# DLRM tower: one one-hot pick of 256 columns for two tiles, and six tiles of single-row fetches on SyncE

## The chip, the cores and the metric

One core of one Trainium2 chip. The metric is the device time of one execution in microseconds; the runs of the kernel before have a median of 560.53 us. Below, PE is TensorE, DVE is VectorE, ACT is ScalarE, POOL is GpSimd and SP is SyncE.

## What is computed

A recommendation tower over a batch of 2048 samples. Each sample has 27 ids; each id takes one row of 128 floats from its own table. The 27 rows, all 351 dot products between two different rows, and 16 dense values go through three layers in float32.

```python
def reference(dense_ctx, ids, tbl_0, ..., tbl_26, W_top1, b_top1, W_top2, b_top2, W_top3):
    e = jnp.stack([tbl_0[ids[:, 0]], ..., tbl_26[ids[:, 26]]], axis=1)   # 2048 x 27 x 128
    inter = jnp.einsum('bfd,bgd->bfg', e, e)[:, _TRIU_I, _TRIU_J]        # 351 pairs
    h = jnp.concatenate([e.reshape(B, -1), inter, dense_ctx], axis=1)    # 3823 wide
    h = jnp.maximum(h @ W_top1 + b_top1, 0.0)                            # 512
    h = jnp.maximum(h @ W_top2 + b_top2, 0.0)                            # 256
    return h @ W_top3
```

## The kernel before

The batch is cut into 16 tiles (0 to 15) of 128 samples. A tile has 9 groups of 3 features (FEATS = 3, GROUPS = 9). For each group the work goes through four engines:

- **POOL** gathers the rows of one feature for 128 samples with one indirect DMA (L320). The result goes to a ring of 6 group slots (RING), so a group's gathers may start once the group six places earlier has been transposed (L317). POOL does nothing else.
- **PE** transposes the three 128x128 blocks into a PSUM bank (L638), two items ahead of the item whose layer 1 it computes. It adds the group's part of layer 1 in three passes (L668 to L670): each float32 operand is split in a high and a low part of type float32r, and high x high, high x low and low x high are summed. Layer 1 of an item waits for the split (`group_low_done`).
- **ACT** writes the high part (L344) and a whole copy for the pair products (L351).
- **DVE** subtracts to get the low part (L469).

The order of the items is written out by hand: SEQUENCE is groups 0 to 6, then "pairs" (the interactions of the tile before), then groups 7 and 8. So the transposes of group 8 stand on PE in front of the layer 1 of "pairs". The pair products (L735), layer 2 and the last layer of earlier tiles are spread between the items. The last tile has a sequence of its own. p_group has two banks of four 128-column places, of which a group uses three.

Not all rows come through POOL:

- Feature 26 (PICKED) has a table of 1000 rows, which lies split in SBUF. For tiles 2 to 14 DVE compares the tile's 128 ids with the row numbers (`make_pick`, L543, once a tile), which gives a one-hot matrix of 1000 x 128, and PE multiplies the table with it in 16 matmuls of 128 columns (L625, L626), in front of the transposes of group 8.
- Feature 25 (FETCHED) comes through SP in the tiles 5, 8, 11 and 14 (FETCH_TILES). SP loads 16 ids into registers (L272), then issues 16 DMAs of one row each (L276), and so on for 128 rows. A tile's rows are split into three parts of 48, 48 and 32 rows, issued in three successive tiles' time (FETCH_PARTS), into one of two buffers (`fetched`). PE transposes them last in group 8 (L642), behind the wait for `rows_fetched`.

SP's queue runs in its written order. It loads the weights in 34 pieces through STAGES = 4 staging buffers; piece n waits until n - 3 pieces have been split (`w_low_done`, L245). Then for each tile from 2 on, it issues the load of the dense values (`load_ctx`, L261, which waits for `ctx_used` of an earlier tile), the load of the tile's ids for the pick (`load_pick_ids`, L279), and one part of the row fetches:

```python
            for t in range(PICK_FROM, TILES):
                load_ctx(t)
                if t < LAST:
                    load_pick_ids(t)
                if (t - 2) // 3 < len(FETCH_TILES):
                    fetch_rows((t - 2) // 3, (t - 2) % 3)
```

"(t, g)" below means group g of tile t.

Of the kernel before, what the change touches and what calls it, by code (L numbers as in the profile page):

```python
# [30 lines left out]
def dlrm_tower(nc, ids, ids_rows, fetch_ids, table_row, tables, ctx_rows, w_dense, w_pairs, b1_t, w2, b2, w3, eye, out):  # L31
# [27 lines left out]
    WIDE = NF + WRAP  # L59
    STAGES = 4  # L60

# [9 lines left out]
    picked_t = ids_rows.rearrange("(t b) -> t b", b=P)  # L71

    FETCHED = NF - 2
    FETCH_TILES = [5, 8, 11, 14]
    FETCH_PARTS = [0, 48, 96, P]
    FETCH_ROWS = tables[FETCHED].shape[0]
    LOADED = 16

    def picked_in(t):
        return PICK_FROM <= t < LAST  # L80

    def gathers_in(t, g):
        return FEATS - (g == GROUPS - 1) * (picked_in(t) + (t in FETCH_TILES))

# [4 lines left out]
    with ExitStack() as ctx:  # L89
# [19 lines left out]
        with ExitStack() as late:  # L109
            def later(name, shape, dt):  # L110
                return late.enter_context(nc.sbuf_tensor(name, shape, dt))

            pick = later("pick", [PICK_ROWS, PICK_CHUNKS, P], F32R)
            pick_ids = [later(f"pick_ids_{k}", [PICK_ROWS, P], I32) for k in range(2)]
            hid2 = later("hid2", [P, HID2], F32)
        stage_room = sb("stage_room", [P, STAGES, HID1])
        table_high = sb("table_high", [PICK_ROWS, PICK_CHUNKS, D], F32R)
        table_low = sb("table_low", [PICK_ROWS, PICK_CHUNKS, D], F32R)
        fetched = sb("fetched", [P, 2, D])
        table_row_sb = sb("table_row_sb", [PICK_ROWS, PICK_CHUNKS], I32)  # L120

# [20 lines left out]
        y = sb("y", [P, P])  # L142
        y_rows = sb("y_rows", [TILES, P])

# [11 lines left out]
        ctx_loaded = [sem(f"ctx_loaded_{k}") for k in range(2)]  # L156
        pick_ids_loaded = [sem(f"pick_ids_loaded_{k}") for k in range(2)]
        y_stored = sem("y_stored")
# [52 lines left out]
        def bank_of(t, n):  # L211
            return p_group[ORDER.index((t, n)) % 2][:, 0:FEATS, :]

        def occupant_before(t, n):
            return ORDER[ORDER.index((t, n)) - 2]
# [26 lines left out]
        def _(sp):  # L242
# [17 lines left out]

            def load_ctx(t):  # L261
                wait(sp, ctx_used, t - 1)
                sp.dma_start(ctx_sb[:, t % 2, :], ctx_t[:, t, :]).then_inc(ctx_loaded[t % 2], 16)
# [15 lines left out]
            def load_pick_ids(t):  # L279
                wait(sp, pick_done, t - PICK_FROM - 1)  # L280
                sp.dma_start(pick_ids[t % 2][:], picked_t[t].partition_broadcast(PICK_ROWS)).then_inc(
                    pick_ids_loaded[t % 2], 16)

            sp.dma_start(idx[:, 0:1, :], ids_t[:, 0:1, :]).then_inc(ids_loaded[0], 16)
# [12 lines left out]

            sp.wait_ge(w_low_done, len(STAGED))
            for t in range(PICK_FROM, TILES):
                load_ctx(t)  # L300
# [9 lines left out]
        def _(pool):  # L310
            pool.wait_ge(ids_loaded[0], 16)
            for t in range(TILES):
                if t == 1:
                    pool.wait_ge(ids_loaded[1], 16)
                for g in range(GROUPS):
                    slot = ring_slot(t, g)
                    wait(pool, group_transposed, t * GROUPS + g - RING + 1)  # L317
                    for k in range(gathers_in(t, g)):
                        f = g * FEATS + k
                        pool.indirect_dma_start(  # L320
                            gathered[:, slot, k, :], None, tables[f],
                            bass.IndirectOffsetOnAxis(ap=idx[:, t, f:f + 1], axis=0),
                        ).then_inc(group_gathered[slot], 16)

        @block.scalar
        def _(act):
            def weight_high(n):
# [11 lines left out]
                nc.scalar.activation(dst, src, ACT.Copy).then_inc(w_high_done, 1)  # L339

            def copy_high(t, g):
                s = t * GROUPS + g
                wait(act, group_used, s - SPLIT + 1)
                nc.scalar.activation(emb_high[:, s % SPLIT, :, :], bank_of(t, g),  # L344
                                     ACT.Copy).then_inc(group_high_done, 1)

            def copy_whole(t, g):
                if g == 0:
                    wait(act, round_done, (t - 1) * ROUNDS)
                f0 = g * FEATS  # L350
                nc.scalar.activation(emb[t % 2][:, :, f0:f0 + FEATS].rearrange("p b f -> p f b"),  # L351
                                     bank_of(t, g), ACT.Copy).then_inc(group_copied, 1)

            def group_copies(t, g):
# [7 lines left out]
                else:  # L362
                    copy_high(t, g)
                    copy_whole(t, g)

            def copy_first(t, r):
# [48 lines left out]
            for k, (t, n) in enumerate(ORDER):  # L415
# [28 lines left out]
        def _(dve):  # L444
# [17 lines left out]
            def group_low(t, g):  # L462
                s = t * GROUPS + g
                if t == 0:
                    for n in range(FEATS * g, FEATS * (g + 1)):
                        weight_low(n)
                dve.wait_ge(group_high_done, s + 1)
                dve.wait_ge(group_copied, s + 1)
                nc.vector.tensor_tensor(emb_low[:, s % SPLIT, :, :], bank_of(t, g),  # L469
                                        emb_high_f32[:, s % SPLIT, :, :], ALU.subtract).then_inc(group_low_done, 1)  # L470

# [63 lines left out]

            def make_pick(t):

                dve.wait_ge(pick_ids_loaded[t % 2], ((t - PICK_FROM) // 2 + 1) * 16)
                dve.wait_ge(w_low_done, len(STAGED))
                wait(dve, pick_used, t - PICK_FROM)  # L540
                rows = table_row_sb[:].unsqueeze(2).broadcast_to([PICK_ROWS, PICK_CHUNKS, P])
                ids_b = pick_ids[t % 2][:].unsqueeze(1).broadcast_to([PICK_ROWS, PICK_CHUNKS, P])
                nc.vector.tensor_tensor(pick[:], ids_b, rows, ALU.is_equal).then_inc(pick_done, 1)  # L543

# [16 lines left out]
            for k, (t, n) in enumerate(ORDER):  # L561
# [43 lines left out]
        def _(pe):  # L605
# [10 lines left out]
            def landings(t, g):  # L616

                groups = range((t * GROUPS + g) % RING, t * GROUPS + g + 1, RING)
                return sum(gathers_in(n // GROUPS, n % GROUPS) for n in groups)

            def pick_rows(t, dst):

                pe.wait_ge(pick_done, t - PICK_FROM + 1)
                for c in range(PICK_CHUNKS):
# [5 lines left out]
            def transpose_group(t, g):  # L630

                slot = ring_slot(t, g)
                wait_for_bank(t, g)
                if g == GROUPS - 1 and picked_in(t):
                    pick_rows(t, bank_of(t, g)[:, FEATS - 1, :])
                pe.wait_ge(group_gathered[slot], landings(t, g) * 16)
                for k in range(gathers_in(t, g)):
                    last = nc.tensor.transpose(bank_of(t, g)[:, k, :], gathered[:, slot, k, :], identity[:])  # L638
# [33 lines left out]
            def layer1_group(t, g, feats=range(FEATS)):  # L672
                s = t * GROUPS + g
                if g == 0:
                    wait(pe, hid1_copied, t - 1)
                pe.wait_ge(group_low_done, s + 1)
                for k in feats:
# [3 lines left out]
                    last = three_passes(p_hid1[t % 2][:], emb_high[:, s % SPLIT, k, :], emb_low[:, s % SPLIT, k, :],  # L681
                                        w1_high[:, f, :], w1_low[:, f, :], f == 0, False)
                if feats[-1] == FEATS - 1:
# [167 lines left out]
```

## Time and profile before

| | |
|---|---|
| Median of 3 runs | 560.53 us (556.34 to 561.19) |
| The profiled execution | 559.26 us |
| Its span, first to last instruction | 557.5 us |
| PE busy | 522.9 us (94%) |
| POOL busy | 399.2 us (72%) |
| ACT busy, DVE busy | 255.6 us (46%), 243.9 us (44%) |
| Gathers on POOL, single-row fetches on SP | 415, 512 |

The profile is of one execution. Its span is shorter than its device time by 559.26 - 557.5 = 1.8 us, which lie around the first and the last instruction. Busy time of PE is time in which at least one matmul was in flight; since matmuls overlap, the distance between the starts of two of them says what one costs. A matmul that waits shows as idle time in front of it. SP shows only when it issues: its row in the timeline merges issues of one line and gives their count. The page writes the names of buffers without their numbers.

### The profile page before, as it was taken

What the parts mean: (1) busy time and instruction counts of PE and PEld (TensorE: products, weight loads), DVE (VectorE), ACT (ScalarE), POOL (GpSimd) and SP (SyncE); (2) the same over time, 40 slices, a digit from 0 to 9 for tenths busy, and PEclk for the clock granted to TensorE, in tenths of its full rate; (3) what the DMA queues carried; (4) which work ended last, traced back from release to release, by engine and by line L of the source; (5) the groups of instructions that cost most, each with busy time, mean ns of one, the idle gap of its engine ahead of it and who ended that gap; (6) DMA issues with size and microseconds to landing.
All of it is one profiled execution on the core that took longest, in us unless ns stands there. A gap on an engine that the chain in (4) does not pass through costs nothing.

```text
span 557.5 us, 12647 instructions
## 1 busy us (share of the span) xinstructions
PE 522.9 (94%) x4420; PEld 429.9 (77%) x4420; DVE 243.9 (44%) x491; ACT 255.6 (46%) x488; POOL 399.2 (72%) x419
## 2 busy tenths in 40 slices
PE   0769889999999999999999999999999999999996
PEld 0547668878788788888888888888888888888884
DVE  3563533436254352534435253443525344352544
ACT  3674545353353535435353543535354353533542
POOL 6777777777777777777777777777777777777600
PEclk9998999999999999999999999999999999999999
DMA  6784321212112112211212121221212122111100
GB/s 171 257 256 130 110 54 57 57 54 60 53 56 59 55 54 56 60 54 57 59 54 59 54 59 54 58 61 55 59 54 59 53 57 60 55 53 54 53 2 1
DMA packets 27041, 38.80 MB, mean 70 GB/s; under 512 B 12455, under 2 KB 16504, under 8 KB 26978
## 3 DMA queue, kind: packets, MB, share of 16 engines
q0 software_dynamic: 13280, 27.22, 17.6%
q1 hardware_dynamic: 13698, 10.77, 6.7%
q8 instruction: 35, 0.57, 0.4%
q14 instruction: 28, 0.23, 0.1%
HBM read 37.96 MB, written 0.01 MB: 68 GB/s over the span
## 4 chain that ended last, share of the span: by engine, by line
PE 72%; POOL 17%; issue 6%; DMA 3%; ACT 1%; DVE 0%; DVEq 0%; ACTq 0%; POOLq 0%
POOL gathered L320 17%; PE p_hid L668 17%; PE p_hid L670 16%; PE p_hid L669 16%; PE p_prod L735 10%; PE p_group L638 7%; DMA gathered<-tbl_dram,idx 3%; PE p_group L626 1%; PE p_group L625 1%; PE p_hid_t L700 1%; PE p_group L655 1%; DMA idx<-ids_dram 0%; ACT emb L351 0%; PE p_hid L735 0%; PE p_hid_t L735 0%
## 5 line engine op out<-in xcount | busy, mean ns | idle before, releaser
L320 POOL DMA_INDIRECT gathered<-tbl_dram,idx x415 | 399.0, 961 | 128.5 <-issue 118.9
L668 PE MATMUL p_hid<-w_high,emb_high 128*128 128x512 f32 x432 | 183.6, 425 | 0.0
L670 PE MATMUL p_hid<-w_high,emb_low 128*128 128x512 f32 x432 | 171.0, 396 | 0.0
L669 PE MATMUL p_hid<-w_low,emb_high 128*128 128x512 f32 x432 | 169.7, 393 | 0.0
L469 DVE TENSOR_TENSOR emb_low<-p_group,emb_high 128x384 fp32r<-128x384 f32 x144 | 80.3, 558 | 195.3 <-ACT emb L351 194.8
L344 ACT ACTIVATE emb_high<-p_group 128x384 fp32r<-128x384 f32 x144 | 70.7, 491 | 161.3 <-PE p_group L638 145.3
L351 ACT ACTIVATE emb<-p_group 128x384 f32<-128x384 f32 x144 | 125.4, 871 | 0.0
L638 PE MATMUL p_group<-identity,gathered 128*128 128x128 f32 x415 | 73.2, 284 | 28.8 <-DMA gathered<-tbl_dram,idx 28.8
L670 PEld LDWEIGHTS p_hid<-w_high,emb_low 128*128 128x128 f32 x432 | 81.7, 189 | 19.4
L669 PEld LDWEIGHTS p_hid<-w_low,emb_high 128*128 128x128 f32 x432 | 82.5, 191 | 12.9
L668 PEld LDWEIGHTS p_hid<-w_high,emb_high 128*128 128x128 f32 x432 | 82.1, 190 | 12.4
L477 DVE COPY prod<-p_prod 32x216 f32<-32x216 f32 x124 | 47.3, 382 | 90.8 <-ACT prod L370 88.8
L638 PEld LDWEIGHTS p_group<-identity,gathered 128*128 128x128 f32 x415 | 48.0, 142 | 43.1 <-issue 21.6
L735 PEld LDWEIGHTS p_prod<-emb 128*64 128x64 f32 x1984 | 62.8, 138 | 22.7 <-issue 21.5
L735 PE MATMUL p_prod<-emb 128*64 128x54 f32 x1984 | 70.7, 224 | 1.0 <-ACT emb L351 1.0
L370 ACT ACTIVATE prod<-p_prod 128x216 f32<-128x216 f32 x62 | 21.8, 351 | 93.9 <-PE p_prod L735 88.2
L460 DVE TENSOR_TENSOR w_low<-w_stage,w_high 128x512 fp32r<-128x512 f32 (+1 forms) x32 | 21.6, 689 | 11.1 <-ACT w_high L339 10.9
L339 ACT ACTIVATE w_high<-w_stage 128x512 fp32r<-128x512 f32 (+1 forms) x32 | 20.1, 636 | 12.4 <-DMA w_stage<-w_dense_dram 11.8
L626 PE MATMUL p_group<-pick,table_low 125*128 125x128 f32 x104 | 23.9, 275 | 0.0
L625 PE MATMUL p_group<-pick,table_high 125*128 125x128 f32 x104 | 23.2, 268 | 0.0
L668 PE MATMUL p_hid<-w_high,inter_high 126*128 126x512 f32 x48 | 20.4, 425 | 0.2 <-DVE table_low L460 0.2
L626 PEld LDWEIGHTS p_group<-pick,table_low 125*128 125x128 f32 x104 | 19.9, 192 | 0.6
(73 smaller groups left out, 358.6 us busy)
## 6 DMA issues: line engine op xcount, KB each, us to landing
fetched<-tbl_dram SPq DMA_DIRECT2D x512, 0.5 KB
w_stage<-w_dense_dram SPq DMA_DIRECT2D x27, 256.0 KB, 3.6
gathered<-tbl_dram,idx POOLq DMA_INDIRECT x415, 2.5
pick_ids<-ids_rows_dram SPq DMA_DIRECT2D x13, 62.5 KB
w_stage<-w_pairs_dram SPq DMA_DIRECT2D x3, 252.0 KB
w_stage<-w_dram SPq DMA_DIRECT2D x2, 256.0 KB, 3.8
w_stage<-tbl_dram SPq DMA_DIRECT2D x2, 250.0 KB
ctx_sb<-ctx_rows_dram SPq DMA_DIRECT2D x16, 13.5 KB
```

The source lines that it names most:

```text
L320: pool.indirect_dma_start(gathered[:, slot, k, :], None, tables[f], bass.IndirectOffsetOnAxis(ap=idx[:, t, f:f + 1], axis=0),).then_inc(gr ...
L344: nc.scalar.activation(emb_high[:, s % SPLIT, :, :], bank_of(t, g), ACT.Copy).then_inc(group_high_done, 1)
L351: nc.scalar.activation(emb[t % 2][:, :, f0:f0 + FEATS].rearrange("p b f -> p f b"), bank_of(t, g), ACT.Copy).then_inc(group_copied, 1)
L469: nc.vector.tensor_tensor(emb_low[:, s % SPLIT, :, :], bank_of(t, g), emb_high_f32[:, s % SPLIT, :, :], ALU.subtract).then_inc(group_low_d ...
L477: nc.vector.tensor_copy(round_columns(r)[rows], round_products(t, r)[rows, 1]).then_inc(second_copied, 1)
L625: nc.tensor.matmul(dst, table_high[:, c, :], pick[:, c, :], start=c == 0, stop=False)
L626: last = nc.tensor.matmul(dst, table_low[:, c, :], pick[:, c, :], start=False, stop=c == PICK_CHUNKS - 1)
L638: last = nc.tensor.transpose(bank_of(t, g)[:, k, :], gathered[:, slot, k, :], identity[:])
L668: nc.tensor.matmul(dst, high, w_high, start=start, stop=False)
L669: nc.tensor.matmul(dst, high, w_low, start=False, stop=False)
L670: return nc.tensor.matmul(dst, low, w_high, start=False, stop=stop)
L735: last = nc.tensor.matmul(bank[h * 2 * SLOT:(h + 1) * 2 * SLOT, j * 2 * NF:(j + 1) * 2 * NF], x.rearrange("p b f -> p (b f)"), x[:, :, 0:N ...
```

## The change

- **Pick.** `make_pick` fills a one-hot matrix of 256 columns for an even tile and the odd one after it, in two halves (at items 4 and 5 of the even tile). PE runs its 16 matmuls once for two tiles, with 256 columns, in group 8 of the even tile; the odd tile's feature 26 lands in the fourth place of the bank. ACT copies it out in two more instructions (`copy_next`), DVE computes its low part into `next_low`, and layer 1 of the odd tile reads it from there. In the odd tile group 8's copies and subtraction handle two features. Tile 14 is no longer picked: POOL gathers its feature 26.
- **Fetches.** FETCH_TILES is 3, 5, 8, 10, 12, 14, and the parts are gone: SP issues the rows of six tiles one after the other. From the third on, a tile's fetch first waits until the fetch two before it has been transposed.
- **SP's other loads.** The dense values and the pick's ids are issued from ACT's queue. SP no longer waits for all weights to be split before it fetches.
- **Buffers.** STAGES is 5, so that weight piece n waits until n - 4 pieces are split; y_rows and the pick's buffers lie over others, and the scratch of the dynamic DMAs is 2048 instead of 4096 bytes.

```diff
-    STAGES = 4
+    STAGES = 5
...
+    PICK_TO = TILES - 2
...
-    FETCH_TILES = [5, 8, 11, 14]
-    FETCH_PARTS = [0, 48, 96, P]
+    FETCH_TILES = [3, 5, 8, 10, 12, 14]
...
-            pick = later("pick", [PICK_ROWS, PICK_CHUNKS, P], F32R)
-            pick_ids = [later(f"pick_ids_{k}", [PICK_ROWS, P], I32) for k in range(2)]
+            pick = later("pick", [PICK_ROWS, PICK_CHUNKS, 2 * P], F32R)
+            pick_ids = later("pick_ids", [PICK_ROWS, 2 * P], I32)
...
-            def fetch_rows(n, part):
+            def fetch_rows(n):
 
                 t = FETCH_TILES[n]
-                if part == 0 and n >= 2:
+                if n >= 2:
                     sp.wait_ge(group_transposed, FETCH_TILES[n - 2] * GROUPS + GROUPS)
-                for b in range(FETCH_PARTS[part], FETCH_PARTS[part + 1], LOADED):
+                for b in range(0, P, LOADED):
...
-            sp.wait_ge(w_low_done, len(STAGED))
-            for t in range(PICK_FROM, TILES):
-                load_ctx(t)
-                if t < LAST:
-                    load_pick_ids(t)
-                if (t - 2) // 3 < len(FETCH_TILES):
-                    fetch_rows((t - 2) // 3, (t - 2) % 3)
+            for n in range(len(FETCH_TILES)):
+                fetch_rows(n)
...
+            def load_ctx(t):
+                act.wait_ge(ctx_used, t - 1)
+                act.dma_start(ctx_sb[:, t % 2, :], ctx_t[:, t, :]).then_inc(ctx_loaded[t % 2], 16)
+
+            def load_pick_ids(t):
+                act.wait_ge(w_low_done, len(STAGED))
+                wait(act, pick_done, t - PICK_FROM)
+                act.dma_start(pick_ids[:], picked_t[t // 2].partition_broadcast(PICK_ROWS)).then_inc(pick_ids_loaded, 16)
...
+            def copy_next(t):
+
+                if t > PICK_FROM:
+                    act.wait_ge(group_used, t * GROUPS)
+                nc.scalar.activation(next_high[:], next_bank_of(t), ACT.Copy).then_inc(next_high_done, 1)
+                act.wait_ge(round_done, t * ROUNDS)
+                nc.scalar.activation(emb[(t + 1) % 2][:, :, PICKED], next_bank_of(t), ACT.Copy).then_inc(next_copied, 1)
...
+                if n == 6 and 2 <= t + 1 < TILES:
+                    load_ctx(t + 1)
+                if n == 7 and picks_start(t + 1):
+                    load_pick_ids(t + 1)
...
+                if g == GROUPS - 1 and picks_start(t):
+                    dve.wait_ge(next_high_done, (t - PICK_FROM) // 2 + 1)
+                    dve.wait_ge(next_copied, (t - PICK_FROM) // 2 + 1)
+                    nc.vector.tensor_tensor(next_low[:], next_bank_of(t), next_high[:].bitcast(F32),
+                                            ALU.subtract).then_inc(next_low_done, 1)
...
-                if n == 4 and PICK_FROM <= t < LAST:
-                    make_pick(t)
+                if n in (4, 5) and picks_start(t):
+                    make_pick(t, n - 4)
...
-                if g == GROUPS - 1 and picked_in(t):
-                    pick_rows(t, bank_of(t, g)[:, FEATS - 1, :])
+                if g == GROUPS - 1 and picks_start(t):
+                    pick_rows(t, p_group[ORDER.index((t, g)) % 2][:, FEATS - 1:FEATS + 1, :])
...
-    nc = bacc.Bacc("TRN2", target_bir_lowering=False, num_devices=1, dynamic_dma_scratch_size=4096)
+    nc = bacc.Bacc("TRN2", target_bir_lowering=False, num_devices=1, dynamic_dma_scratch_size=2048)
```

In SP's queue, the place behind the weights. Before, the loads of dense values (L263) and ids (L281) stand ahead of the first fetch, whose three id instructions are L272 and whose rows are L276:

```order
12 L259 DMA w_stage<-w2_dram 128x2x256 [waits w_low_done] x2
13 L259 DMA w_stage<-tbl_26_dram 125x4x128 [waits w_low_done] x2
14 L263 DMA ctx_sb<-ctx_rows_dram 128x27 [waits ctx_used,w_low_done]
15 L281 DMA pick_ids_0<-ids_rows_dram 125x128
16 L272 TENSOR_LOAD fetch_ids_dram_ptr
17 L272 REGISTER_ALU
18 L272 TENSOR_LOAD fetch_ids_dram
19 L276 ISA
20 L276 DMA fetched<-tbl_25_dram 1x128
```

The same place after the change (line numbers are those of the changed kernel):

```order
12 L280 DMA w_stage<-w2_dram 128x2x256 [waits w_low_done] x2
13 L280 DMA w_stage<-tbl_26_dram 125x4x128 [waits w_low_done] x2
14 L289 TENSOR_LOAD fetch_ids_dram_ptr
15 L289 REGISTER_ALU
16 L289 TENSOR_LOAD fetch_ids_dram
17 L293 ISA
18 L293 DMA fetched<-tbl_25_dram 1x128
```

The two loads and their waits have left the queue. A block of 16 rows has the same instructions as before; there are 48 blocks instead of 32.

In PE's queue, the transposes of (14, 8) before the change, behind 16 pick matmuls of which the last two are shown:

```order
2110 L625 MATMUL p_group_0<-pick,table_high 128x128
2111 L626 MATMUL p_group_0<-pick,table_low 128x128
2112 L638 MATMUL p_group_0<-identity,gathered 128x128 [waits group_gathered_2]
2113 L642 MATMUL p_group_0<-identity,fetched 128x128 [waits rows_fetched_1]
2114 L668 MATMUL p_hid1_1<-w1_high,inter_high 128x512 [waits inter_low_done]
```

And after it:

```order
2000 L678 MATMUL p_group_0<-identity,gathered 128x128 [waits group_gathered_2,inter_low_done]
2001 L678 MATMUL p_group_0<-identity,gathered 128x128
2002 L682 MATMUL p_group_0<-identity,fetched 128x128 [waits rows_fetched_1]
2003 L708 MATMUL p_hid1_1<-w1_high,inter_high 128x512 [waits inter_low_done]
```

The pick has left tile 14, one gathered block has come in its place, and the transpose of the fetched rows still stands in front of everything else that PE has to do.

## Rows read from the trace of the kernel before

**Rows 1.** The page's first part: busy us, share, instructions.

```profile
PE 522.9 (94%) x4420; PEld 429.9 (77%) x4420; DVE 243.9 (44%) x491; ACT 255.6 (46%) x488; POOL 399.2 (72%) x419
```

**Rows 2.** Busy time in stretches: stretch, length, PE, PEld, DVE, ACT, POOL, clock, DMA.

```profile
105.00:140.00 35.00, 34.53 (x290) 28.46 (x289) 14.72 (x30) 15.27 (x30) 26.76 (x28) 1.00 0.22 58
...
315.00:350.00 35.00, 35.00 (x321) 29.38 (x322) 14.68 (x30) 15.61 (x31) 26.47 (x29) 1.00 0.21 57
```

**Rows 3.** POOL: its longest wait (us, times, longest), and its last gather (start, us).

```profile
POOL gathered L320 <- issue: 118.9, 390, 0.3
...
527.00 0.94 POOL L320 DMA_INDIRECT gathered<-tbl_dram,idx  x1 [0.30 <-issue]
```

**Rows 4.** Timeline of PE: the transposes of the fetched rows of (5, 8) and (14, 8).

```profile
209.91 0.27 PE L642 MATMUL p_group<-identity,fetched 128*128 128x128 f32 x1
...
502.99 0.27 PE L642 MATMUL p_group<-identity,fetched 128*128 128x128 f32 x1
```

**Rows 5.** Timeline of SP's queue: start, us, line, what, count of issues.

```profile
58.46 4.27 SPq L259 DMA_DIRECT2D w_stage<-tbl_dram  x2
...
75.78 0.32 SPq L281 DMA_DIRECT2D pick_ids<-ids_rows_dram  x1
79.30 25.87 SPq L276 DMA_DIRECT2D fetched<-tbl_dram  x48
...
105.65 0.32 SPq L281 DMA_DIRECT2D pick_ids<-ids_rows_dram  x1
109.70 26.00 SPq L276 DMA_DIRECT2D fetched<-tbl_dram  x48
...
136.16 0.32 SPq L281 DMA_DIRECT2D pick_ids<-ids_rows_dram  x1
139.62 16.14 SPq L276 DMA_DIRECT2D fetched<-tbl_dram  x32
...
200.66 0.32 SPq L281 DMA_DIRECT2D pick_ids<-ids_rows_dram  x1
205.47 26.00 SPq L276 DMA_DIRECT2D fetched<-tbl_dram  x48
```

**Rows 6.** The fetch's instructions on SP: count, ns min/median/max, first and last.

```profile
L272 SPq TENSOR_LOAD <-fetch_ids_dram_ptr x32: 1082/1146/2210, 76.1 to 439.4; - x32
...
L272 SPq TENSOR_LOAD <-fetch_ids_dram x32: 1707/1718/1949, 77.4 to 440.7; - x32
...
L276 SPq DMA_DIRECT2D fetched<-tbl_dram x512: 224/225/303, 79.3 to 448.8; - x171
```

**Rows 7.** Landings: issues, KB each, median us from issue to landing.

```profile
gathered<-tbl_dram,idx POOLq DMA_INDIRECT x415, 2.5
...
idx<-ids_dram SPq DMA_DIRECT2D x1, 13.5 KB, 1.7
```

**Rows 8.** Columns as in rows 2: a lowered clock and the stretch ahead of it.

```profile
35.00:40.00 5.00, 3.04 (x14) 1.90 (x13) 3.63 (x6) 4.07 (x9) 3.96 (x4) 1.00 0.80 242
40.00:45.00 5.00, 3.85 (x12) 3.09 (x12) 3.10 (x5) 2.95 (x6) 3.79 (x4) 0.66 0.81 249
```

**Rows 9.** Timeline of PE: first and last pick matmul of tile 14, two 256-column matmuls.

```profile
501.12 0.22 PE L625 MATMUL p_group<-pick,table_high 125*128 125x128 f32 x1
...
502.74 0.28 PE L626 MATMUL p_group<-pick,table_low 125*128 125x128 f32 x1
...
525.80 0.28 PE L669 MATMUL p_hid<-w_low,hid_high 128*128 128x256 f32 x1
525.92 0.28 PE L670 MATMUL p_hid<-w_high,hid_low 128*128 128x256 f32 x1
```

**Rows 10.** Groups by line: the pick on DVE: busy us, mean ns, idle before.

```profile
L543 DVE TENSOR_TENSOR pick<-pick_ids,table_row_sb 125x1024 fp32r<-125x1024 int32 x13 | 16.1, 1235 | 0.0
```

**Rows 11.** Timeline of PE: the last tile's group 8, the last one transposed.

```profile
536.18 0.49 PE L638 MATMUL p_group<-identity,gathered 128*128 128x128 f32 x3
```

More of the change, by code:

```diff
@@ L79, in picked_in, with picks_start, picked_before, gathered_feats @@
     def picked_in(t):
-        return PICK_FROM <= t < LAST
-    def gathers_in(t, g):
-        return FEATS - (g == GROUPS - 1) * (picked_in(t) + (t in FETCH_TILES))
+        return PICK_FROM <= t < PICK_TO
+    def picks_start(t):
+        return picked_in(t) and t % 2 == 0
+    def picked_before(t):
+        return picked_in(t) and t % 2 == 1
+    def gathered_feats(t, g):
+        if g < GROUPS - 1:
+            return range(FEATS)
+        return [k for k in range(FEATS) if not (g * FEATS + k == PICKED and picked_in(t))
+                and not (g * FEATS + k == FETCHED and t in FETCH_TILES)]
     ids_t = ids.rearrange("(t p) f -> p t f", p=P)
@@ L119, in dlrm_tower @@
         fetched = sb("fetched", [P, 2, D])
+        next_high = sb("next_high", [P, P], F32R)
+        next_low = sb("next_low", [P, P], F32R)
         table_row_sb = sb("table_row_sb", [PICK_ROWS, PICK_CHUNKS], I32)
@@ L156, in dlrm_tower @@
         ctx_loaded = [sem(f"ctx_loaded_{k}") for k in range(2)]
-        pick_ids_loaded = [sem(f"pick_ids_loaded_{k}") for k in range(2)]
+        pick_ids_loaded = sem("pick_ids_loaded")
+        next_high_done = sem("next_high_done")
+        next_copied = sem("next_copied")
+        next_low_done = sem("next_low_done")
         y_stored = sem("y_stored")
@@ L212, in bank_of, with next_bank_of, feats_in @@
             return p_group[ORDER.index((t, n)) % 2][:, 0:FEATS, :]
+        def next_bank_of(t):
+            return p_group[ORDER.index((t, GROUPS - 1)) % 2][:, FEATS, :]
+        def feats_in(t, g):
+            return FEATS - 1 if g == GROUPS - 1 and picked_before(t) else FEATS
         def occupant_before(t, n):
@@ L317, in _ @@
                     wait(pool, group_transposed, t * GROUPS + g - RING + 1)
-                    for k in range(gathers_in(t, g)):
+                    for k in gathered_feats(t, g):
                         f = g * FEATS + k
@@ L350, in copy_whole @@
                 f0 = g * FEATS
-                nc.scalar.activation(emb[t % 2][:, :, f0:f0 + FEATS].rearrange("p b f -> p f b"),
-                                     bank_of(t, g), ACT.Copy).then_inc(group_copied, 1)
+                n = feats_in(t, g)
+                nc.scalar.activation(emb[t % 2][:, :, f0:f0 + n].rearrange("p b f -> p f b"),
+                                     bank_of(t, g)[:, 0:n, :], ACT.Copy).then_inc(group_copied, 1)
             def group_copies(t, g):
@@ L534, in last_hid1_split, with make_pick @@
                                             ALU.subtract).then_inc(hid1_low_done, 1)
[L536 to L540, printed above, removed]
+            def make_pick(t, half):
+                if half == 0:
+                    dve.wait_ge(pick_ids_loaded, ((t - PICK_FROM) // 2 + 1) * 16)
+                    wait(dve, pick_used, (t - PICK_FROM) // 2)
+                columns = slice(half * P, (half + 1) * P)
                 rows = table_row_sb[:].unsqueeze(2).broadcast_to([PICK_ROWS, PICK_CHUNKS, P])
-                ids_b = pick_ids[t % 2][:].unsqueeze(1).broadcast_to([PICK_ROWS, PICK_CHUNKS, P])
-                nc.vector.tensor_tensor(pick[:], ids_b, rows, ALU.is_equal).then_inc(pick_done, 1)
+                ids_b = pick_ids[:, columns].unsqueeze(1).broadcast_to([PICK_ROWS, PICK_CHUNKS, P])
+                nc.vector.tensor_tensor(pick[:, :, columns], ids_b, rows, ALU.is_equal).then_inc(pick_done, 1)
             def layer3(t):
@@ L618, in landings @@
                 groups = range((t * GROUPS + g) % RING, t * GROUPS + g + 1, RING)
-                return sum(gathers_in(n // GROUPS, n % GROUPS) for n in groups)
+                return sum(len(gathered_feats(n // GROUPS, n % GROUPS)) for n in groups)
             def pick_rows(t, dst):
-                pe.wait_ge(pick_done, t - PICK_FROM + 1)
+                pe.wait_ge(pick_done, t - PICK_FROM + 2)
                 for c in range(PICK_CHUNKS):
@@ L633, in transpose_group @@
                 wait_for_bank(t, g)
-                if g == GROUPS - 1 and picked_in(t):
-                    pick_rows(t, bank_of(t, g)[:, FEATS - 1, :])
+                if g == GROUPS - 1 and picks_start(t):
+                    pick_rows(t, p_group[ORDER.index((t, g)) % 2][:, FEATS - 1:FEATS + 1, :])
                 pe.wait_ge(group_gathered[slot], landings(t, g) * 16)
-                for k in range(gathers_in(t, g)):
+                for k in gathered_feats(t, g):
                     last = nc.tensor.transpose(bank_of(t, g)[:, k, :], gathered[:, slot, k, :], identity[:])
@@ L676, in layer1_group @@
                 pe.wait_ge(group_low_done, s + 1)
+                if g == GROUPS - 1 and picked_before(t):
+                    pe.wait_ge(next_low_done, (t - 1 - PICK_FROM) // 2 + 1)
                 for k in feats:
@@ L680, in layer1_group @@
                         pe.wait_ge(w_low_done, f + 1)
-                    last = three_passes(p_hid1[t % 2][:], emb_high[:, s % SPLIT, k, :], emb_low[:, s % SPLIT, k, :],
-                                        w1_high[:, f, :], w1_low[:, f, :], f == 0, False)
+                    if k < feats_in(t, g):
+                        high, low = emb_high[:, s % SPLIT, k, :], emb_low[:, s % SPLIT, k, :]
+                    else:
+                        high, low = next_high[:], next_low[:]
+                    last = three_passes(p_hid1[t % 2][:], high, low, w1_high[:, f, :], w1_low[:, f, :], f == 0, False)
                 if feats[-1] == FEATS - 1:
```

23 lines of the change are left out of this document (10 added, 13 removed).

## The prediction

> **What bounds the kernel now.** I read the page's first part and found PE busy for 94% of the span [rows 1]. A share is a mean over stages, so next came the table of stretches [rows 2]. At 105 to 140 us PE still has gaps (34.53 of 35 us); at 315 to 350 it has none. Either another engine feeds PE just fast enough, or PE is behind it. POOL's waits decide that: its longest is "issue", 118.9 us in 390 pieces of 0.3 us, which is the distance between two gathers and no wait for anybody [rows 3]. POOL runs freely, one gather every 0.94 + 0.30 = 1.25 us, to its last one at 527.00 [rows 3]. Nothing on POOL can make it end earlier than that, except fewer gathers.
>
> PE and POOL are nearly equal. From the transpose of the fetched rows of (5, 8) to that of (14, 8) are nine tiles and 502.99 - 209.91 = 293.1 us, 32.6 us a tile [rows 4]. POOL needs 26 gathers in most tiles, 26 x 1.25 = 32.5 us. The last tile's group 8 is transposed at 536.18 [rows 11], well behind the landing of the last gather (527.00 + 2.5 = 529.5) [rows 3, 7], so at the end PE is the later of the two, by some 7 us. DVE and ACT are busy for 15 to 16 us of 35 [rows 2] and bound nothing.
>
> Last I read SP's queue, since the change gives it more to do. It isn't counted as busy anywhere, and only its timeline shows it [rows 5].
>
> **SP's fetches: the term that decides.** A part of a fetch begins as soon as the id load of the pick is issued. Part one begins at 75.78 + 0.32 = 76.10 and its 48 rows are issued by 79.30 + 25.87 = 105.17: 29.07 us. Part two: 105.97 to 135.70, 29.73 us. Part three, 32 rows: 136.48 to 155.76, 19.28 us [rows 5]. So a tile of 128 rows takes SP 29.07 + 29.73 + 19.28 = 78.1 us of pure issuing, with no wait in it. That is 8 blocks of 9.76 us: two loads of ids (1.15 + 1.72 = 2.9 us) and 16 rows at about 0.43 us, of which the DMA instruction itself is 0.225 [rows 6]. The blocks are made of the same instructions after the change, so I take 78.1 us a tile. "Without pause" removes the time between the parts, not the 78.1.
>
> Two more tiles cost two times 78.1 us, in a queue that so far had room. Does it have room for six? The start moves forward. Before, the two halves of the small table are loaded at 58.46 and some 4 us later, each waiting for one more split piece [rows 5]. With five staging buffers the second half waits for the count that the first waited for, so it goes at 58.46 and takes 0.3 us. SP then fetches at once, at 58.8, since the wait for all pieces is gone too. Six tiles: 58.8 + 6 x 78.1 = 527.4 us. The last rows land 1.7 us after their issue, by the load of ids, the smallest of the landings in the rows (from 0 to 2.5, the gather's, is possible) [rows 7]: 529.1 us.
>
> The rows for tile n of the list are thus there at 60.5 + 78.1 n: 138.6, 216.7, 294.8, 372.9, 451.0, 529.1. PE wanted those of (5, 8) at 209.91 and those of (14, 8) at 502.99; by 32.6 us a tile (3, 8), (8, 8), (10, 8), (12, 8) lie at 144.8, 307.6, 372.7, 437.8. So tile 3 is in time, 5 is late by 7, 8 in time, 10 just about, 12 late by 13, and 14 late by 26 us. SP's own waits for `group_transposed` (of the fetch two before) are met 60 us or more before SP comes to them, so SP is held up by nobody and 529.1 stands whatever PE does meanwhile.
>
> What is queued behind that wait on PE: everything. The transpose of the fetched rows stands in front of the layer 1 of "pairs" of tile 14, and the whole rest of the program. That rest took 557.48 - 502.99 = 54.5 us with PE nearly always busy [rows 4], and its instructions are the same: 529.1 + 54.5 = 583.6 us. POOL doesn't add to it. By its ring it may run up to (15, 4) and then stands until (14, 8) is transposed; its last 12 gathers then end at 529.1 + 12 x 1.25 + 2.5 = 546.6, and PE comes to the last of them 536.18 - 502.99 = 33.2 us after the wait, at 562 [rows 4, 11].
>
> **The clock.** PE stands for some 15 us before it resumes (it comes from (12, 8) at 451 and needs about 62 us for two tiles). In the rows the granted clock fell to a mean of 0.66 in a stretch of 5 us, behind one in which PE was busy for 3.04 of 5 us only [rows 8]. With the levels 1.2 and 2.4 GHz that is 0.34 x 5 / 0.5 = 3.4 us at the low one, and 1.7 us lost. I add 1.7 once, for the last wait; the earlier ones are hidden by the waits that follow. None and twice as much are the bounds.
>
> **Sum.** 58.8 + 468.6 + 1.7 + 54.5 + 1.7 = 585.3 us of span. The profiled execution was 559.26 against a span of 557.5, so 1.8 lie outside it: 587.1, **587 us**. The median before is 1.3 above that execution and another run 3 below it, so I correct for neither.
>
> **The other edits,** which the wait above hides. *Pick on PE:* 16 matmuls of 128 columns lie 1.62 / 15 = 0.11 us apart, 1.7 us a tile; 256 columns cost 0.12 [rows 9], 1.9 us for two tiles. 13 x 1.7 - 6 x 1.9 = 10.7, less a transpose: PE is relieved of some 10.5 us, about 7.7 of it behind (5, 8). It goes into waiting for SP. *POOL:* 12 gathers less for the pick and 6 for the fetches, from 432, is 414 instead of 415: 1.25 us. *DVE and ACT:* as many halves of a pick as picks were, less one (1.24 us each [rows 10]), but two in one tile; and for each pair of tiles two copies and one subtraction more, 0.5 us each by the mean of their instructions (255.6 / 488, 243.9 / 491) [rows 1]. Both have over half of each stretch free [rows 2]. If that cover were gone it would be 1.24 + 1.5 = 2.7 us a pair, 16 us in all. *ACT's two DMA issues:* 0.3 to 0.4 us a tile in the same free time; their waits were met several items earlier. *Scratch of 2048 bytes:* a gather lands after 2.5 us, two distances of POOL, so few are under way at once [rows 3, 7]. I take zero; the bound above is in the rivals.
>
> **A page that speaks against the sum.** The row is: 0.225 us for the DMA instruction of one fetched row, 512 times, never under 0.224 [rows 6]. The Trainium skill, DMA: Bandwidth & Descriptors, in the section on the anatomy of one DMA, puts the sequencer's dispatch at about 50 ns. By that, an estimate, a row would take 0.43 - 0.225 + 0.05 = 0.25 us, a block 7.0 and a tile 56 us; SP would be done in time and the first rival below would hold. The page speaks of the path by GpSimd there, and this trace does not agree with it for SP.
>
> **Rivals.**
> - *SP keeps up: faster.* Point from which it decides: PE, relieved, would want (14, 8) at about 503.0 - 7.7 = 495.3. SP makes that if a tile takes (495.3 - 60.5) / 6 = 72.5 us or less. For it speaks that about 0.43 a row is more than the 0.225 of the instruction, so there are gaps that might close; if all closed, a block were 2.9 + 16 x 0.225 = 6.5 us and a tile 52. Against it: no part shows a pace under 9.6 us a block [rows 5]. Then the end goes by POOL: 527.00 - 1.25 + 2.5 = 528.3 for the last landing, or PE 536.18 - 7.7 = 528.5, and 557.5 - 536.2 = 21.3 behind it [rows 3, 11]: 549.8 + 1.8 = 551.6 us. Chance 0.06.
> - *SP is late by a part:* a pace between 72.5 and 76 us ends between 552 and 574 us. Chance 0.05, of which 0.02 below 555.
> - *SP is slower than in its first tile.* The part from 200.98 to 231.47 took 30.49 us [rows 5]; a tile of such parts is 8 x 30.49 / 3 = 81.3 us, and the end 6 x 3.2 = 19 us later, 606. It speaks for it that some loads of ids took 2.2 us instead of 1.1 [rows 6], against it that the median is 1.15. Chance 0.05.
> - *Shorter scratch holds POOL:* if each gather had to wait until the one before had landed, 414 x 2.5 = 1035 us. Nothing shows POOL near a limit. Chance 0.02.
> - *The change doesn't pause less:* if the waits for `group_transposed` held SP, it would end later still. By the times above they are met; this is in the slow rival.
>
> **How the numbers follow.** Forecast 0.82, rivals 0.06, 0.05, 0.05, 0.02. Inside the forecast a tile of 76.5 to 79.5 us makes -10 to +8, the landing -1.7 to +0.8, the clock +-1.7: 574 to 598. The range reaches a little into both neighbours, 571 to 601. A measurement of this kernel can tell about 1% from no change; 555 and 566 are those limits. Faster than that 0.07, within it 0.03, slower 0.90.
>
> **What would show it.** Right: SP's fetched rows follow each other from about 59 to 527 us with no wait; PE has waits at the fetched transposes of tiles 5, 12 and 14, of about 7, 14 and 15 us; POOL waits for PE for the first time, some 12 to 15 us before (15, 5); from the last fetched transpose to the end are 54 to 57 us; the pick's matmuls are 0.12 apart. Wrong: SP done by 495; or a longest wait of PE that is on DVE, ACT or a gather; or gathers more than 1.25 us apart.

## The result: 5.7% slower, set by SyncE's fetches

The changed kernel takes 591.29 us (median of 5 runs, 589.57 to 594.51), the kernel before 560.53 us. The ratio is 1.057, 95% interval 1.054 to 1.060. Forecast were 587 us and a range of 571 to 601.

The profiled execution took 594.51 us, its span is 592.7. It is the slowest of the five; the spans of the other four are 587.7 to 590.1 us. The first part of its page and the chain of work that ended last:

```profile
PE 518.3 (87%) x4309; PEld 424.3 (72%) x4309; DVE 242.7 (41%) x496; ACT 255.7 (43%) x500; POOL 400.2 (68%) x418
...
SPq 52%; PE 23%; issue 16%; POOL 5%; DMA 2%; ACT 1%; DVE 1%; DVEq 0%; ACTq 0%; POOLq 0%
SPq L293 32%; SPq L289 20%; PE p_hid L708 6%; PE p_hid L710 5%; PE p_hid L709 5%; POOL gathered L328 5%; PE p_prod L780 3%; PE p_group L678 2%; DMA gathered<-tbl_dram,idx 1%; PE p_hid_t L745 0%; DMA fetched<-tbl_dram 0%; ACT emb L378 0%; DMA idx<-ids_dram 0%; PE p_group L695 0%; ACT emb_high L362 0%
```

PE has less work than in [rows 1] and a smaller share. The chain now goes through an engine that the first line doesn't list: SP's issues of rows (L293, 32% of the span) and its loads of ids (L289, 20%) make up half of it. SP's queue in the timeline, and the loads of ids one by one (count, ns min/median/max, first and last start):

```profile
58.82 3.93 SPq L280 DMA_DIRECT2D w_stage<-tbl_dram  x2
67.31 466.78 SPq L293 DMA_DIRECT2D fetched<-tbl_dram  x768
```

```profile
L289 SPq TENSOR_LOAD <-fetch_ids_dram_ptr x48: 1072/1112/2445, 62.8 to 524.7; - x48
...
L289 SPq TENSOR_LOAD <-fetch_ids_dram x48: 1700/1754/2617, 65.4 to 525.8; - x48
```

One stretch without a pause: from the first load at 62.8 to 67.31 + 466.78 = 534.1 are 471.3 us, 78.5 us a tile, against 78.1 from [rows 5]. An issue still takes 0.225 us at the median, and the loads are as long as in [rows 6]. What PE sees of it, in its timeline (in brackets the idle time ahead and what ended it):

```profile
143.68 0.33 PE L682 MATMUL p_group<-identity,fetched 128*128 128x128 f32 x1 [0.84 <-DMA fetched<-tbl_dram]
...
222.01 0.48 PE L682 MATMUL p_group<-identity,fetched 128*128 128x128 f32 x1 [14.54 <-DMA fetched<-tbl_dram]
...
383.68 0.27 PE L682 MATMUL p_group<-identity,fetched 128*128 128x128 f32 x1
...
457.49 0.47 PE L682 MATMUL p_group<-identity,fetched 128*128 128x128 f32 x1 [10.31 <-DMA fetched<-tbl_dram]
...
535.10 0.48 PE L682 MATMUL p_group<-identity,fetched 128*128 128x128 f32 x1 [13.52 <-DMA fetched<-tbl_dram]
```

The rows are those of tiles 3, 5, 10, 12 and 14; the long waits are those of 5, 12 and 14. Compare the last with [rows 4]: (14, 8) is transposed 32.1 us later. POOL now has long waits for PE as well; its longest, in its timeline, ends right behind that transpose:

```profile
535.85 0.94 POOL L328 DMA_INDIRECT gathered<-tbl_dram,idx  x1 [10.25 <-PE p_group L682]
```

### The profile page after: what moved, and what is told of

The parts are those of the page before. It is cut to its first block, busy times and chain, and to the rows that moved or that the text cites. A ratio compares the mean times of both kernels' runs of the same rounds, so it can differ in the third digit from the quotient of the medians.

```text
span 592.7 us, 13258 instructions
## 1 busy us (share of the span) xinstructions
PE 518.3 (87%) x4309; PEld 424.3 (72%) x4309; DVE 242.7 (41%) x496; ACT 255.7 (43%) x500; POOL 400.2 (68%) x418
## 4 chain that ended last, share of the span: by engine, by line
SPq 52%; PE 23%; issue 16%; POOL 5%; DMA 2%; ACT 1%; DVE 1%; DVEq 0%; ACTq 0%; POOLq 0%
SPq L293 32%; SPq L289 20%; PE p_hid L708 6%; PE p_hid L710 5%; PE p_hid L709 5%; POOL gathered L328 5%; PE p_prod L780 3%; PE p_group L678 2%; DMA gathered<-tbl_dram,idx 1%; PE p_hid_t L745 0%; DMA fetched<-tbl_dram 0%; ACT emb L378 0%; DMA idx<-ids_dram 0%; PE p_group L695 0%; ACT emb_high L362 0%
## 5 line engine op out<-in xcount | busy, mean ns | idle before, releaser
L708 PE MATMUL p_hid<-w_high,emb_high 128*128 128x512 f32 x426 | 181.6, 426 | 0.0
L710 PE MATMUL p_hid<-w_high,emb_low 128*128 128x512 f32 x426 | 168.8, 396 | 0.0
L709 PE MATMUL p_hid<-w_low,emb_high 128*128 128x512 f32 x426 | 167.9, 394 | 0.0
L678 PEld LDWEIGHTS p_group<-identity,gathered 128*128 128x128 f32 x414 | 50.0, 144 | 43.1 <-issue 28.3
L780 PEld LDWEIGHTS p_prod<-emb 128*64 128x64 f32 x1984 | 62.8, 138 | 22.6 <-issue 21.4
L682 PE MATMUL p_group<-identity,fetched 128*128 128x128 f32 x6 | 2.3, 382 | 39.2 <-DMA fetched<-tbl_dram 39.2
L708 PE MATMUL p_hid<-w_high,inter_high 126*128 126x512 f32 x48 | 22.6, 471 | 0.2 <-DVE table_low L493 0.2
L709 PE MATMUL p_hid<-w_low,inter_high 126*128 126x512 f32 x48 | 21.1, 440 | 0.0
## 6 DMA issues: line engine op xcount, KB each, us to landing
ctx_sb<-ctx_rows_dram ACTq DMA_DIRECT2D x14, 13.5 KB
```

The lines of the kernel that those rows point to most:

```text
L708: nc.tensor.matmul(dst, high, w_high, start=start, stop=False)
L709: nc.tensor.matmul(dst, high, w_low, start=False, stop=False)
L710: return nc.tensor.matmul(dst, low, w_high, start=False, stop=stop)
L780: last = nc.tensor.matmul(bank[h * 2 * SLOT:(h + 1) * 2 * SLOT, j * 2 * NF:(j + 1) * 2 * NF], x.rearrange("p b f -> p (b f)"), x[:, :, 0:N ...
```

## The experiments

Each kernel was compared with the kernel before on the same chip; its median there lay between 559.3 and 560.2 us. Times are medians, ratios have their 95% interval.

### SP's part alone: fetch_only

The kernel before with this edit, and the loads of dense values and ids on ACT's queue:

```diff
-    FETCH_TILES = [5, 8, 11, 14]
-    FETCH_PARTS = [0, 48, 96, P]
+    FETCH_TILES = [3, 5, 8, 10, 12, 14]
...
-            sp.wait_ge(w_low_done, len(STAGED))
-            for t in range(PICK_FROM, TILES):
...
+            for n in range(len(FETCH_TILES)):
+                fetch_rows(n)
```

> The kernel before (pick of 128 columns for each tile, STAGES 4, scratch 4096) with only SP's part of the change: six tiles without pause, dense values and ids on ACT's queue. Theory: SP alone sets the end, so it is as slow as the whole change, 587 to 594 us; SP's first fetch starts near 59 to 63 and the last row is issued near 530 to 534; PE's waits in front of the fetched rows are shorter than in the changed kernel because PE arrives later. Rival (the pick has a share in the loss): 560 to 580 us.

Measured: 597.16 us, ratio 1.068 (1.064 to 1.072). It keeps the old pick, the four staging buffers and the old scratch, and it is as slow: SP's part alone is enough for the whole loss. SP's fetches and PE's last wait for them, in the timelines:

```profile
69.71 467.65 SPq L271 DMA_DIRECT2D fetched<-tbl_dram  x768
```

```profile
538.35 0.47 PE L641 MATMUL p_group<-identity,fetched 128*128 128x128 f32 x1 [10.91 <-DMA fetched<-tbl_dram]
```

The last row is issued at 537.4, 3.3 us later than in the changed kernel, of which 2.1 come from a first load at 64.9 instead of 62.8. PE arrives later, as expected, and waits 10.9 us instead of 13.5; the span ends 2.6 us later than the changed kernel's. The median is 3 us above the range that I gave.

### The old list in the changed kernel: four_tiles, and old_pick_four

```diff
-    FETCH_TILES = [3, 5, 8, 10, 12, 14]
+    FETCH_TILES = [5, 8, 11, 14]
```

> The changed kernel with the old list of fetched tiles (5, 8, 11, 14), all else as changed. Theory (SP's six fetches are the whole loss): SP has each tile's rows long before PE wants them, POOL makes 416 gathers and sets the end: last gather starts at about 528.2, + 2.5 landing + 21.3 behind it + 1.8 outside the span = 554 us, ratio about 0.99, no wait of PE on fetched rows. Rival (the pick of 256 columns, its copies or the smaller scratch cost time of their own): 560 us or more, ratio 1.00 to 1.03, with PE waiting for DVE or gathers further than 1.25 us apart.

Measured: 558.89 us, ratio 0.998 (0.996 to 1.000). The loss is gone and no wait for fetched rows is left. But the gain that I expected, 1%, is not there either. The same list with the old pick:

> The kernel before with SP fetching its four tiles (5, 8, 11, 14) without pause and the dense values and ids on ACT's queue; the pick as before. Theory: no part of this was on the path, 415 gathers, 558 to 561 us, ratio within 0.995 to 1.005; PE has no gaps behind 240 us. Against the run four_tiles (558.9, pick of 256 columns, 416 gathers) it shows what the pick brings: 1 to 2 us, because POOL's pace takes the rest. Rival (the two extra DMA issues on ACT hold its copies up): 563 us or more.

Measured: 559.07 us, ratio 0.998 (0.996 to 1.001). So the pick of 256 columns, with its copies, halves, fifth staging buffer, smaller scratch and the one gather more that tile 14 costs (416 instead of 415), brings nothing that these runs can tell. But it does relieve PE. PE's waits for gathers behind 210 us, in the waits of four_tiles (us, times, longest):

```profile
PE p_group L678 <- DMA gathered<-tbl_dram,idx: 7.1, 8, 1.8
```

old_pick_four has no such wait there.

### Five tiles, and six where SP has them in time: five_tiles, six_spread, six_repeat

```diff
-    FETCH_TILES = [3, 5, 8, 10, 12, 14]
+    FETCH_TILES = [3, 6, 8, 11, 13]
```

> The changed kernel with five fetched tiles placed behind what SP needs for one (3, 6, 8, 11, 13). Theory: rows are ready at about 142, 221, 299, 378, 456 us and wanted later than that except for a few us, so no wait of PE on fetched rows over 2 us; POOL makes 415 gathers, 552 to 554 us. Rival (any continuous fetching on SP disturbs POOL's gathers or PE): as slow as six tiles, over 575 us.

Measured: 558.14 us, ratio 0.997 (0.995 to 0.999). A wait of 1.15 us at tile 3 is all that is left; the time is 4 us above the forecast. With `[3, 6, 8, 11, 13, 15]`:

> The changed kernel with six tiles where SP has the rows in time or nearly (3, 6, 8, 11, 13, 15), the same number of rows and of gathers (414) as the change. Theory: rows are ready at about 142, 221, 299, 378, 456, 535; only the last, wanted at about 532, is late, by 3 us or so; 558 to 563 us. Rival (it is the number of row fetches that costs, wherever they stand): about 590 us.

Measured: 556.31 us, ratio 0.995 (0.992 to 0.997). This is the decisive run on the cause. It is 2 us below its forecast, and PE waits for no fetched row. It issues the same 768 rows as the change, at the same pace (78.4 us a tile, from 60.3 to 530.8), and makes the same 414 gathers; only the tiles are placed so that the rows are there when PE wants them. 35 us lie between the two. The run was repeated:

> The run six_spread once more, on the same chip as seven_sbuf: 555 to 557 us, ratio 0.992 to 0.997; the wait for tile 15's rows at most 3 us.

Measured: 557.82 us, ratio 0.998 (0.995 to 1.001), a little above the forecast. The wait for tile 15's rows, in the timeline:

```profile
533.33 0.33 PE L682 MATMUL p_group<-identity,fetched 128*128 128x128 f32 x1 [2.14 <-DMA fetched<-tbl_dram]
```

The two runs' intervals overlap; that this list is faster than the kernel before is not certain.

### A late tile in the middle: no_tile_14

The changed kernel with `[3, 5, 8, 10, 12]`.

> The changed kernel with the first five of its six tiles (3, 5, 8, 10, 12). Theory: the wait at (12, 8) stays (about 10 us, until 457 us), and what PE has behind it then sets the end: 119.7 us in the kernel before, less 3.4 for the pick of tiles 13 and 14, plus about 2 of clock: 457 + 118.5 + 1.8 = 577 us. So the loss is bounded by the last late tile, at 1 for 1. Rival (a late tile in the middle is caught up, only tile 14 costs): 560 us or less.

Measured: 575.22 us, ratio 1.027 (1.022 to 1.032). The last late tile decides, as the wait in the timeline shows:

```profile
454.87 0.48 PE L682 MATMUL p_group<-identity,fetched 128*128 128x128 f32 x1 [10.11 <-DMA fetched<-tbl_dram]
```

From 454.87 to the end of the span, 574.0, are 119.1 us, against an estimate of 118.5 + 1.8. Nothing of that wait is caught up. PE's work behind it fills the time.

### SP's pace: load_32, ids_in_sbuf2, sbuf_32

Three runs change only how SP gets the ids; list and rows are those of the change. First 32 ids at a time (`LOADED = 32`):

> The changed kernel, six tiles, but 32 ids loaded into SP's registers at a time instead of 16, so that half of the id loads go (24 blocks instead of 48). Theory: a tile takes SP 4 x (3.0 + 32 x 0.43) = 67 us instead of 78.5, under the 72.5 at which SP keeps up; rows are ready at 131, 198, 265, 332, 399, 466; no long wait of PE on them; POOL's 414 gathers set the end: 550 to 553 us, ratio 0.98 to 0.99. Rival (the time goes by rows issued or by landings and not by the id loads): a tile stays near 78 us and the end near 590.

Measured: 559.82 us, ratio 0.999 (0.997 to 1.002). The loads, and PE at tiles 5 and 14:

```profile
L289 SPq TENSOR_LOAD <-fetch_ids_dram_ptr x24: 1086/1112/2537, 61.0 to 482.1; - x24
...
L289 SPq TENSOR_LOAD <-fetch_ids_dram x24: 3351/3572/3953, 63.7 to 483.5; - x24
```

```profile
67.81 432.86 SPq L293 DMA_DIRECT2D fetched<-tbl_dram  x768
```

```profile
210.27 0.33 PE L682 MATMUL p_group<-identity,fetched 128*128 128x128 f32 x1 [2.91 <-DMA fetched<-tbl_dram]
...
501.80 0.48 PE L682 MATMUL p_group<-identity,fetched 128*128 128x128 f32 x1 [3.72 <-DMA fetched<-tbl_dram]
```

A load of 32 ids takes 3.57 us and one of 16 takes 1.75: it costs by the id. Only the load of the pointer in front of it (1.11 us) costs once. So a tile takes (500.7 - 61.0) / 6 = 73.3 us and not the 67 that I had expected, just above the threshold of 72.5, and two short waits are left. 5.2 us less a tile turned 591 into 560.

The short wait at tile 14 costs more than its 3.7 us. Stretches of this run behind it (columns as in [rows 2]):

```profile
502.00:507.00 5.00, 5.00 (x15) 3.93 (x15) 1.25 (x2) 1.44 (x3) 3.78 (x5) 0.50 0.20 52
507.00:508.00 1.00, 1.00 (x4) 0.83 (x3) 0.00 (x0) 1.00 (x2) 0.70 (x2) 0.64 0.03 8
```

PE works without a gap, but at the lower clock for 5.9 us, from 501.8 on, which is some 3 us lost. So a wait of 3.7 us cost nearly 7. The missed forecast (550 to 553) has this in it, and the price of the rival, which the last part comes to.

Then the ids in SBUF, in columns of `y` that nothing reads; the pointer's load goes:

```diff
+            def load_fetch_ids(n):
+                if n == 0:
+                    sp.wait_ge(zeroed, 3)
+                for q in range(0, P, 32):
+                    at = FETCH_TILES[n] * P + q
+                    sp.dma_start(y[q:q + 1, 16 + 32 * (n % 3):48 + 32 * (n % 3)].bitcast(I32),
+                                 fetch_ids[at:at + 32].unsqueeze(0)).then_inc(fetch_ids_loaded[n % 2], 16)
...
-                        fetch_ids[at:at + LOADED].unsqueeze(0), engines=[mybir.EngineType.SP], min_val=0, max_val=FETCH_ROWS - 1,
+                        y[q:q + 1, at:at + LOADED].bitcast(I32), engines=[mybir.EngineType.SP], min_val=0, max_val=FETCH_ROWS - 1,
```

> The changed kernel, six tiles (3, 5, 8, 10, 12, 14), 16 ids at a time, but the ids lie in SBUF (free columns of y) and SP loads them from there, so that the load of a pointer goes. Theory (the time goes by SP's pace alone, threshold some 72 us a tile): a tile takes SP at most 78.5 - 8 x 1.15 = 69 us, perhaps less if a load from SBUF is shorter than 1.75; no wait of PE on fetched rows over 2 us, 555 to 559 us, as with four or five tiles. Rival (more rows in flight on SP's queue slow other things): 565 us or more though the rows are in time.

Measured: 555.35 us, ratio 0.992 (0.990 to 0.995), the fastest median of the study and below both kernels: six tiles in the very places of the change, with only SP's way to the ids changed. Its loads, and SP's last fetches:

```profile
L300 SPq TENSOR_LOAD <-y x48: 1136/1230/1378, 65.7 to 445.0; - x48
```

```profile
327.17 125.94 SPq L304 DMA_DIRECT2D fetched<-tbl_dram  x256
```

One load of 1.23 us has taken the place of two of 2.87. From 65.7 to 327.17 + 125.94 = 453.1 are 64.6 us a tile, under the bound that I gave. PE waits for no fetched row.

> As ids_in_sbuf2 with 32 ids at a time: tells what a load from SBUF costs once and by id. If it costs by id, a tile takes SP the same; if it costs once, 4 loads less a tile.

Measured: one single run, of 556.15 us, too little for a ratio. A load of 32 ids from SBUF takes 2.12 us, one of 16 1.23: that is 0.34 once and 0.056 for each id, against 0.11 for each id from DRAM.

### Seven tiles: seven_sbuf

ids_in_sbuf2 with `FETCH_TILES = [3, 5, 7, 9, 11, 13, 15]`.

> ids_in_sbuf2 with seven fetched tiles (3, 5, 7, 9, 11, 13, 15). SP took 64.6 us a tile there and started near 65.7: rows are ready at about 131, 196, 260, 325, 390, 454, 519 and wanted at 143, 207, 272, 337, 402, 467, 530, so all are in time. Theory: POOL makes 413 gathers and the last tile's last group has one gather less: 552 to 555 us, faster than all kernels so far. Rival (POOL is no longer what PE waits for near the end, PE's own work in the last two tiles is): as ids_in_sbuf2, 555 us.

Measured: 556.48 us, ratio 0.993 (0.991 to 0.996). The rival held: a tile more for SP and a gather less for POOL bring nothing over six. PE's last wait for a gather and POOL's last gather:

```profile
503.67 0.52 PE L692 MATMUL p_group<-identity,gathered 128*128 128x128 f32 x3 [1.18 <-DMA gathered<-tbl_dram,idx]
```

```profile
526.53 0.96 POOL L342 DMA_INDIRECT gathered<-tbl_dram,idx  x1 [0.30 <-issue]
```

POOL's last gather starts at 526.53 instead of 528.13 in ids_in_sbuf2, and the span is 554.8 instead of 554.2 us. The profiled execution has a lowered clock near the end that the one of ids_in_sbuf2 lacks (a stretch of seven_sbuf, then of ids_in_sbuf2):

```profile
548.00:552.00 4.00, 2.79 (x12) 2.53 (x12) 2.19 (x10) 0.12 (x1) 0.00 (x0) 0.58 0.01 2
```

```profile
548.00:552.00 4.00, 2.15 (x13) 1.79 (x13) 2.66 (x11) 0.43 (x2) 0.00 (x0) 1.00 0.01 2
```

So differences of 1 us between these spans say nothing of the list.

## Why the prediction was right, and where it was off

**SP's pace times six, and PE behind it.** This was the term that decided, and it held. Its sum was 585.3 us of span; the profiled execution has 592.7, the median one 589.5. The 7.4 us to the profiled one are four terms:

- *The start of the fetches, 58.8: measured 62.8, + 4.0.* Each half of the small table did wait for one split piece less. But the first half went at 58.82, not 4 us ahead of [rows 5], and the second 4 us behind it: the pieces themselves were split 4 us later, which ate what the fifth buffer won. The piece that the second half waits for, in DVE's timeline of the changed kernel, is done at 61.75 + 0.68 = 62.43:

```profile
61.75 0.68 DVE L493 TENSOR_TENSOR w_low<-w_stage,w_high 126x512 fp32r<-126x512 f32 x1
```

  In the other runs with five buffers and ids from DRAM the first load lies between 59.2 and 61.9, with four buffers at 64.9 (fetch_only) and 65.2 (old_pick_four). So 58.8 was a little early in every run, and the profiled execution is the worst of them. Why the early stage varies was not settled.
- *Six tiles, 468.6: measured 471.3, + 2.7.* The tile that the forecast read, 78.1 us, was a little quicker than the mean of these six, 78.5; one by one they took 77.6 to 79.8 us.
- *The landing, 1.7: measured 535.1 - 534.1 = 1.0, - 0.7.*
- *The rest of the program with the clock, 54.5 + 1.7: measured 592.7 - 535.1 = 57.6, + 1.4.* The rest itself was as before to some tenths; the clock was dearer than I had put it.

**The clock.** Stretches of the changed kernel: in front of the last wait's end, behind it, and after that (columns as in [rows 2]).

```profile
521.00:535.00 14.00, 0.59 (x4) 0.26 (x2) 0.25 (x1) 0.00 (x0) 3.69 (x4) 0.60 0.08 24
535.00:540.00 5.00, 4.90 (x14) 3.92 (x15) 1.10 (x2) 1.24 (x2) 2.83 (x3) 0.50 0.10 26
540.00:545.00 5.00, 5.00 (x24) 3.81 (x22) 1.27 (x3) 2.51 (x4) 3.75 (x4) 0.90 0.18 52
```

PE was idle for 13.5 us, the granted clock fell to the lower level during the wait, and it stayed there for 5 us of full work and part of the next 5. At 1.2 instead of 2.4 GHz half of that time is lost: 0.50 x 5 + 0.10 x 5 = 3.0 us, where I had 1.7 [rows 8]. Those rows show 3.4 us at the lower level; here it was 5.9 us. The bounds that the forecast gave, none and twice as much, held it. The length of the wait is not the reason: load_32 lost as much behind 3.7 us. Each of the three long waits has such a stretch behind it, but only the last one's counts.

**The waits.** Forecast were 7, 14 and 15 us at tiles 5, 12 and 14; measured 14.5, 10.3 and 13.5. Tile 5's is longer since its rows were there 5 us later than forecast (4.0 of them from the start) and PE came 2.4 us sooner. Tile 12's is shorter: the forecast laid 451 beside a PE that nothing had held up, at 437.8, but the wait at tile 5 had put PE back, and it came to (12, 8) at 457.49 - 10.31 = 447.2. It doesn't matter, as I had said: PE then stands behind tile 5 and takes (8, 8) and (10, 8) when it gets to them, and SP goes on. no_tile_14 shows that the last late tile is paid in full, and fetch_only, with 3.3 us more of lateness and 2.6 us more of span, agrees.

Of the other signs, POOL's wait before (15, 5) was 10.3 us instead of 12 to 15, and it then stood for PE twice more, 1.0 and 3.1 us, so that its last gather began at 553.1 instead of about 543. PE came to the last gathered rows at 571.0 only, so this cost nothing. The last stretch took 57.6 us, just outside the 54 to 57, because of the clock.

**The pick on PE.** The lines of the two forms (mean ns of one, with overlap) in the changed kernel:

```profile
L665 PE MATMUL p_group<-pick,table_high 125*128 125x256 f32 x48 | 11.7, 282 | 0.0
L666 PE MATMUL p_group<-pick,table_low 125*128 125x256 f32 x48 | 11.7, 282 | 0.0
```

Two of them start 0.12 us apart, as [rows 9] had it. The busy time of the two is 23.4 us for 96.

**The rivals.** SP keeps up: in the change it doesn't, and the runs agree with the threshold of 72.5 us a tile: long waits at 78.5 (591 us), short ones at 73.3 (560), none at 64.6 (555). Nothing between 64.6 and 73.3 was tried. What was wrong is the price of that rival, 551.6 us. The step that failed is "Then the end goes by POOL: 527.00 - 1.25 + 2.5 = 528.3 for the last landing, or PE 536.18 - 7.7 = 528.5": in five_tiles PE comes to the last gathered rows at 533.95, only 2.2 us sooner than before. The timeline of PE in five_tiles shows why:

```profile
213.87 0.52 PE L678 MATMUL p_group<-identity,gathered 128*128 128x128 f32 x3 [1.68 <-DMA gathered<-tbl_dram,idx]
...
278.81 0.52 PE L678 MATMUL p_group<-identity,gathered 128*128 128x128 f32 x3 [1.42 <-DMA gathered<-tbl_dram,idx]
...
343.63 0.52 PE L678 MATMUL p_group<-identity,gathered 128*128 128x128 f32 x3 [1.30 <-DMA gathered<-tbl_dram,idx]
...
505.38 0.52 PE L678 MATMUL p_group<-identity,gathered 128*128 128x128 f32 x3 [1.19 <-DMA gathered<-tbl_dram,idx]
```

Behind 210 us there are seven such waits for gathers, 1.68 + 1.42 + 1.30 + 0.67 + 0.15 + 1.14 + 1.19 = 7.6 us, where the kernel before has one of 0.26. A relieved PE overtakes POOL again and again, and nearly all that the pick saves it behind 210 us goes there. That it is the pick is shown by four_tiles and old_pick_four above: 7.1 us of such waits with the new pick, none with the old. From its last such wait, at 505.38, to the end at 555.6 it has 50.2 us of work and never waits for POOL again: the last tile's PE work is longer than POOL's 33 us for it. So neither engine alone sets the end; POOL sets when PE may begin the last tile, and PE sets the rest. This is read from the traces; no run moved POOL's gathers alone. It fits seven_sbuf: its list has six tiles ahead of the last one, as ids_in_sbuf2 has, and the gather that it saves is in the last tile. PE's last wait ends at 503.67 there, against 504.00, and 51.1 us follow, against 50.2.

The scratch of 2048 bytes held nobody up: in the changed kernel a gather took 0.966 us on average against 0.961 before, but in fetch_only, with the old scratch, 0.972. ACT's and DVE's extra work doesn't show at the end: old_pick_four and four_tiles differ by 0.2 us.

## What to carry to other kernels

An issuing queue is an engine with a capacity, though no line of busy time shows it. Count what its longest job costs in its own timeline, multiply by how often it is wanted, and lay the finishing times beside the times at which the consumer wants them; if one lies behind, the last one decides. Here moving the same work to other places (six_spread) and making each piece of it shorter (ids_in_sbuf2) each gave back the whole loss, 35 and 36 us. And a saving on one of two engines that run neck and neck turns into waits for the other.

## What the runs showed of the hardware

- A load of ids from DRAM into SP's registers takes 1.11 us for the pointer and about 0.11 us for each id (1.75 us for 16, 3.57 for 32); from SBUF 0.34 us and 0.056 for each id, with no pointer. For load_32 I had taken it to cost once for each load.
- The 13.5 us of PE's idle time cost 3.0 us more behind it, through the clock that stayed at the lower level for over 5 us of full work. In load_32 an idle time of 3.7 us cost the same.
- 768 DMAs of one row, 0.61 us apart with their share of the loads, left POOL's gathers as they were: in six_spread one took 0.962 us on average, against 0.961 before with 512, and the kernel 556 us.
